# Second-layer attention with heads stacked on 32-row groups, fp32r high/low products, mask rows, and maxima in a two-bank and a one-bank region

## The reference

```python
q = (x @ wq).reshape(B, T, H, D);  lat = x @ w_down
k = (lat @ wk_up).reshape(B, T, H, D);  v = (lat @ wv_up).reshape(B, T, H, D)
q = _apply_rope(q, cos, sin);  k = _apply_rope(k, cos, sin)
scores = einsum('bqhd,bkhd->bhqk', q, k) / sqrt(D)
allowed = (arange(T) // 32)[None, :] <= (arange(T) // 32)[:, None]
attn = softmax(where(allowed, scores, finfo.min))
out = einsum('bhqk,bkhd->bqhd', attn, v).reshape(B, T, E) @ wo
```

## Time and profile before

| | us |
|---|---|
| median of the three runs shown | 2290.97 (2288.64 to 2308.19) |
| the profiled execution | 2288.33 |
| its span, first to last instruction | 2286.5 |

### The profile page before, as it was taken

How to read it: one execution, slowest core, us unless ns; L and a number is a source line. 1 busy time by engine, 2 the same in 40 slices (tenths; PEclk the granted TensorE clock), 3 DMA queues, 4 the chain that set the end, 5 groups by cost and what they waited for, 6 DMA issues and landing times. The chain is left out here.

```text
span 2286.5 us, 39722 instructions
## 1 busy us (share of the span) xinstructions
PE 1803.5 (79%) x11252; PEld 1116.8 (49%) x11300; DVE 1413.4 (62%) x2718; ACT 1200.5 (53%) x1688; POOL 496.7 (22%) x804
## 2 busy tenths in 40 slices
PE   1599999999999999742835719999899994474993
PEld 1366666666666666432832303333333333344993
DVE  4267677766676777641554448788788863522665
ACT  1478778787787777411622203556566662221441
POOL 0112211121122111105410011122122222074441
PEclk9999999999999999955966657999999997586996
DMA  4656666665566666141224541322233202511224
GB/s 168 149 143 151 157 155 156 158 146 144 143 150 157 156 156 153 40 95 49 60 63 177 176 134 32 62 52 48 54 61 61 48 15 96 72 55 49 60 61 129
DMA packets 158933, 239.46 MB, mean 105 GB/s; under 512 B 21691, under 2 KB 107932, under 8 KB 158205
## 3 DMA queue, kind: packets, MB, share of 16 engines
q1 hardware_dynamic: 148102, 222.90, 39.9%
q0 software_dynamic: 6592, 13.56, 1.8%
q10 hardware_dynamic: 4160, 2.10, 0.3%
HBM read 87.18 MB, written 50.17 MB: 60 GB/s over the span
## 5 line engine op out<-in xcount | busy, mean ns | idle before, releaser
L1012 ACT ACTIVATE a_p<-a_score 128x1024 f32<-128x1024 f32 (+3 forms) x384 | 300.7, 810 | 244.4 <-PE a_score L1029 240.4
L1118 DVE TENSOR_REDUCE a_mx<-a_misc 128x1 f32<-128x512 f32 (+3 forms) x768 | 376.3, 548 | 77.8 <-PE a_misc L1060 51.5
L438 ACT ACTIVATE a_p<-a_score 128x1024 f32<-128x1024 f32 (+3 forms) x384 | 290.4, 809 | 182.7 <-PE a_score L464 179.5
L1057 PE MATMUL a_misc<-a_k,a_q 72*128 72x512 bf16 (+3 forms) x768 | 251.7, 349 | 80.8 <-DMA a_v<-values 55.4
L464 PE MATMUL a_score<-a_q,a_kh 128*128 128x512 f32 (+3 forms) x768 | 274.9, 369 | 22.8 <-DMA a_q<-a_stage 19.4
L480 PE MATMUL a_out<-a_p,a_v 128*64 128x512 f32 (+3 forms) x1536 | 290.7, 500 | 0.0
L395 POOL TENSOR_SCALAR_AFFINE_SELECT a_p<-a_p 128x256 f32<-128x256 f32 x256 | 124.0, 514 | 719.4 <-ACT a_p L451 719.4
L451 ACT ACTIVATE a_p<-a_p 128x2560 f32<-128x2560 f32 (+1 forms) x128 | 274.6, 2145 | 1.1
L464 PE MATMUL a_score<-a_q,a_kl 128*128 128x512 f32 (+3 forms) x768 | 254.8, 348 | 0.0
L610 DVE TENSOR_TENSOR a_part<-a_part,a_p 128x1024 f32<-128x1024 f32 (+3 forms) x256 | 224.0, 875 | 8.4 <-ACT a_p L451 1.8
L1029 PE MATMUL a_score<-a_q,a_k 128*128 128x512 bf16 (+3 forms) x720 | 216.0, 327 | 1.9 <-ACT a_p L1012 1.3
(11 more groups left out here) (205 smaller groups left out, 2834.7 us busy)
## 6 DMA issues: line engine op xcount, KB each, us to landing
a_kh<-a_stage SPq DMA_DIRECT2D x128, 256.0 KB, 4.2
a_kl<-a_stage SPq DMA_DIRECT2D x128, 256.0 KB, 4.8
a_q<-a_stage SPq DMA_DIRECT2D x128, 256.0 KB, 5.5
a_xt<-xt SPq DMA_DIRECT2D x32, 512.0 KB
a_q<-qk_parts SPq DMA_DIRECT2D x144, 64.0 KB
a_k<-qk_parts SPq DMA_DIRECT2D x144, 64.0 KB
values<-p_v SPq DMA_DIRECT2D x16, 512.0 KB, 5.3
a_v<-values SPq DMA_DIRECT2D x16, 512.0 KB
```

The source lines that it names most:

```text
L438: nc.scalar.activation(chunk_of(prob[p], c), score_ps[:, c % 2, :, 0:width], ACT.Tanh, scale=scale / clamp).then_inc(tanh_done, 1)
L1012: nc.scalar.activation(prob[s % RING][:, :, 0:width], score_ps[:, s % 2, :, 0:width], ACT.Exp, scale=scale).then_inc(exp_done, 1)
L1057: mm = nc.tensor.matmul(misc[:, bank, 0:keys], q_st[bn][0:ROWS, h, t * P:(t + 1) * P], k_st[bn][0:ROWS, h, key0:key0 + keys], start=True, ...
L1118: nc.vector.tensor_reduce(m[c][:, h, t:t + 1], misc[:, bank, 0:keys], AX_X, ALU.max).then_inc(free, 1)
```

## The change

Queries and keys are split into two parts, high and low, in fp32r (fp32 storage that TensorE takes in one pass) instead of three in bf16. Three products are kept: high by high, high by low, low by high. That is 24 rows a head, then two rows for the maximum's high and low part, then three mask rows: in the keys' stack row g is one for keys of page g+1 or later of each block of 128, in the queries' stack it is a large negative number for the queries of page g. GpSimd makes these eight fixed rows once in `project1` and stores them to DRAM with eight DMAs. A head takes 32 rows, so a quad fills 128 partitions, each head on a row group of its own, and a unit's loads are two DMAs of 512 KB and one of values. Scores and maxima are matmuls on 24 + 2 or, where the mask cuts, 24 + 2 + 3 rows; a block on the diagonal is a matmul of its own of 128 columns. The GpSimd masks and the identity matmuls are gone.

Maxima use two regions instead of three banks in turn: 14 jobs of two heads in two banks, reduced by one VectorE instruction of 1024 elements, and 12 jobs of one head in one bank, which also takes the transposes. VectorE waits per region. Values are multiplied in pairs of chunks, every fourth slot, one pair behind; the exponentials have eight buffers. The output is written by one VectorE instruction per half into an array ordered by quad, and `project_out1` copies it in another order. The load of the stacks waits for the scores, that of the values for the value matmuls.

```diff
-PARTS = 3
+PARTS = 2
+PRODUCTS = ((0, 0), (0, 1), (1, 0))
+MAX_ROW = len(PRODUCTS) * DH1
+MASK_ROW, MASKS = MAX_ROW + PARTS, P // PAGE - 1
+STACK = 32
...
-                        for a in range(PARTS):
-                            dst = of(parts_dram, b)[i * PARTS + a]
-                            sp.dma_start(dst, part[i][:, a, :]).then_inc(stored, 16)
+                        for n, product in enumerate(PRODUCTS):
+                            rows = of(stack_dram, b)[i].rearrange("g (h r) t -> (g h) r t", r=STACK)
+                            sp.dma_start(rows[:, n * DH1:(n + 1) * DH1, :], part[i][:, product[i], :].bitcast(F32))\
+                                .then_inc(stored, 16)
...
+                for i in range(2):
+                    nc.gpsimd.memset(fixed[i][:], float(i)).then_inc(fixed_made, 1)
+                pool.wait_ge(fixed_made, 2)
+
+                nc.gpsimd.affine_select(out=view[0], in_=view[0], compare_op=ALU.not_equal, fill=NEGATIVE, base=PARTS,
+                                        pattern=by_page, channel_multiplier=-1).then_inc(fixed_made, 1)
+                nc.gpsimd.affine_select(out=view[1], in_=view[1], compare_op=ALU.is_ge, fill=0.0, base=PARTS - 1,
+                                        pattern=by_page, channel_multiplier=-1).then_inc(fixed_made, 1)
+                pool.wait_ge(fixed_made, 4)
+                for b in range(BATCH):
+                    for i in range(2):
...
+                        rows = stack_dram[b, i].rearrange("g (h r) t -> r (g h) t", r=STACK)
+                        pool.dma_start(rows[MAX_ROW:STACK], fixed[i][:].to_broadcast([STACK - MAX_ROW, HEADS1, SEQ]))\
+                            .then_inc(fixed_stored, 16)
...
-                        act.wait_ge(rest_done, b * 2 + i + 1)
-                        nc.scalar.copy(part[i][:, 1, :], rest[:]).then_inc(mid_done, 1)
...
-                        nc.vector.tensor_tensor(rest[:], t_cos[:], part[i][:, 0, :], ALU.subtract)\
-                            .then_inc(rest_done, 1)
-                        dve.wait_ge(mid_done, n + 1)
-                        nc.vector.tensor_tensor(part[i][:, 2, :], rest[:], part[i][:, 1, :], ALU.subtract)\
+                        nc.vector.tensor_tensor(part[i][:, 1, :], t_cos[:], part[i][:, 0, :].bitcast(F32), ALU.subtract)\
                             .then_inc(lo_done, 1)
...
+    def jobs(region, pieces):
+        step = 2 if region == WIDE else 1
+        return [(region, range(h, h + step), pieces) for h in range(0, QUAD, step)]
+
+    wide_jobs = [job for pieces in ([(0, 3, 0)], [(2, 4, 0)], [(2, 5, 0)], [(2, 6, 0)], [(2, 7, 0)], [(1, 7, 1)],
+                                    [(0, 1, 0), (1, 5, 1)]) for job in jobs(WIDE, pieces)]
+    narrow_jobs = [job for pieces in ([(0, 0, 0), (1, 4, 1)], [(0, 2, 0)], [(1, 6, 1)]) for job in jobs(NARROW, pieces)]
+    W, N = iter(wide_jobs), iter(narrow_jobs)
+    early_jobs = [next(W if k == "w" else N) for k in "wwnwwnn"]
+    rest_jobs = [next(W if k == "w" else N) for k in "wnwnwnwnwwnwnwnwnwn"]
...
+            todo = []
             if exists(u + 1):
-                left = PIECES if isinstance(u, int) and u == -1 else PIECES[EARLY:]
-                for n, piece in enumerate(left):
-                    by_slot[n * MAX_SLOTS // len(left)].append(("max", (1, *piece), n == len(left) - 1))
-                by_slot[MAX_SLOTS + 2].append(("turn_max", None, None))
-            if exists(u + 2):
-                for n, piece in enumerate(PIECES[:EARLY]):
-                    by_slot[MAX_SLOTS + n * (SLOTS - MAX_SLOTS) // EARLY].append(("max", (2, *piece), False))
+                jobs = (early_jobs if first else []) + rest_jobs
+                todo = [("max", (1, *job), n == len(jobs) - 1) for n, job in enumerate(jobs)]
             if exists(u - 1):
-                by_slot[9].append(("turn_out", 1, None))
+                todo.insert(min(9, len(todo)), ("turn_out", 1, None))
+            for n, use in enumerate(todo):
+                slot = n * MAX_SLOTS // len(todo)
+                by_slot[max(slot, 6) if use[0] == "turn_out" else slot].append(use)
+            todo = [("max", (2, *job), False) for job in early_jobs] if exists(u + 2) else []
+            if exists(u + 1):
+                todo.insert(min(1, len(todo)), ("turn_max", None, None))
             if exists(u):
-                by_slot[15].append(("turn_out", 0, None))
-            n = sum(map(len, by_slot.values()))
-            return by_slot, n
-
-        FULL = len(PIECES) + 3
-
-        def bank_of(u, at):
-
-            short = FULL - uses(u)[1] if isinstance(u, int) and u < 1 else 0
-            return (at + short) % BANKS
+                todo.insert(min(5, len(todo)), ("turn_out", 0, None))
+            for n, use in enumerate(todo):
+                by_slot[MAX_SLOTS + n * (SLOTS - MAX_SLOTS) // len(todo)].append(use)
+            return by_slot
...
+        def load_rows(sp, n, b3):
             if not exists(n):
                 return
-            kit.ge_apart(sp, pv_chunks, (n - BUFS + 1) * NCH)
-            batch, quad = (n >> 2) & (BATCH - 1), n & (QUADS - 1)
-            src = of(parts_dram, batch)
+            kit.ge_apart(sp, scored, (n - BUFS + 1) * SLOTS)
+            src = of(stack_dram, (n >> 2) & (BATCH - 1))
             for which, st in ((0, q_st), (1, k_st)):
-                for a in range(PARTS):
-                    row0 = a * (PARTS * DH1)
-                    for b in range(PARTS):
-                        part = a if which == 0 else b
-                        rows = src[which * PARTS + part].rearrange("(g h d) t -> g d h t", g=QUADS, h=QUAD)
-                        sp.dma_start(st[b3][row0 + b * DH1:row0 + (b + 1) * DH1, :, :], of(rows, quad))\
-                            .then_inc(st_loaded[b3], 16)
-            sp.dma_start(v_st[b3][:], of(of(v_dram, batch), quad)).then_inc(st_loaded[b3], 16)
+                sp.dma_start(st[b3][:].bitcast(F32), of(src[which], n & (QUADS - 1))).then_inc(st_loaded[b3], 16)
+
+        def load_values(sp, n, b3):
+            if not exists(n):
+                return
+            kit.ge_apart(sp, pv_pairs, (n - BUFS + 1) * ROUNDS)
+            sp.dma_start(v_st[b3][:], of(of(v_dram, (n >> 2) & (BATCH - 1)), n & (QUADS - 1))).then_inc(v_loaded[b3], 16)
...
-        def pool_step(pool, u, b3, d3):
-            if not exists(u):
-                return
-            for i in DIAG:
-                for hp in range(2):
-                    slot = 2 * i + hp
-                    kit.ge_apart(pool, exp_done, u * SLOTS + slot + 1)
-                    blk = prob[slot % RING][:, :, 0:P].rearrange("p h (g q) -> p h g q", q=PAGE)
-
-                    nc.gpsimd.affine_select(out=blk, in_=blk, compare_op=ALU.is_ge, fill=0.0, base=PAGE - 1,
-                                            pattern=[[0, 2], [PAGE, P // PAGE], [0, PAGE]], channel_multiplier=-1)\
-                        .then_inc(masked, 1)
...
-    RING = 6
-    PV_LAG = 2
+    RING = 8
+    ROUNDS = NCH // 2
...
+            diagonal = P if j // (TILES // 2) == half else 0
+            for a, b, last_row in ((0, diagonal, MASK_ROW + MASKS), (diagonal, width, MASK_ROW)):
+                if a == b:
+                    continue
+                for h2 in range(2):
+                    row = STACK * (2 * hp + h2)
+                    mm = nc.tensor.matmul(score_ps[:, s % 2, h2, a:b], k_st[b3][row:row + last_row, j * P:(j + 1) * P],
+                                          q_st[b3][row:row + last_row, q0 + a:q0 + b], start=True, stop=True)
+            mm.then_inc(scored, 1)
...
+        def pe_pv(pe, m, b3, pair, loads):
+            if pair == 0:
+                pe.wait_ge(v_loaded[b3], 16 * loads)
+            pe.wait_ge(exp_done, m * SLOTS + 4 * pair + 4)
+            for i in (2 * pair, 2 * pair + 1):
+                half, j, width, _ = CHUNKS[i]
+                if j == 0:
+                    ge(pe, out_evac[1 - half], m + half)
+                last_j = max(c[1] for c in CHUNKS if c[0] == half)
+                for h in range(QUAD):
+                    slot = (2 * i + h // 2) % RING
+                    mm = nc.tensor.matmul(out_ps[h * V_COLS:(h + 1) * V_COLS, HALF - width:HALF],
+                                          v_st[b3][:, j, h, :], prob[slot][:, h % 2, 0:width],
+                                          start=j == 0, stop=j == last_j)
+            mm.then_inc(pv_pairs, 1)
...
-            ge(pe, free, number if isinstance(u, int) and at < BANKS else number - (BANKS - 1))
+            back = back_to_same_region(u, at)
+            if back is not None:
+                ge(pe, free, number - (back - 1))
...
+                            bank = narrow_ps[:] if region == NARROW else wide_ps[:, h % 2, :]
+                            mm = nc.tensor.matmul(bank[:, n * keys + a:n * keys + b],
+                                                  q_st[bn][row:row + last_row, t * P:(t + 1) * P],
```

(22 more changed lines are left out.)

249 lines of the change are left out of this document (110 added, 139 removed).

## The result

The changed kernel takes 2497.3 us (median of 4, 2490.7 to 2501.5) against 2293.8 us (median of 4): ratio 1.087, interval 1.082 to 1.093. It is slower, by more than my range allowed. The profiled execution after took 2498.3 us, its span is 2496.6. These are its busy shares and granted clock, in forty slices.

A forecast was written before the change was run, and what follows sets the result against it. TensorE was taken to bound the loop, with VectorE close behind. From the profiled 2288.3 us, 16 x (34.0 - 31.4) = +42 for the loop, -17 opening and -6 projection gave 2307 us, range 2225 to 2430.

The forecast's parts named there:

- the forecast: Whole kernel: mixed clock in the second layer's attention loop, 34.0 us a unit, 2307 us in all; chance 0.45.
- Opening: Start of second-layer attention: first maxima 17 us earlier through less clearing and fewer loads; net -17 us, bounds -10 to -20.
- Projection: Stage before attention: fewer conversion steps shorten four iterations by 2.1 us each, larger stores add 2; -6 us, bounds -12 and +8.
- Loop, the pairs of values: Attention loop: 6 shape turns a unit instead of 12, 1.2 us instead of 2.4; ScalarE's wait for pairs costs nothing.
- My second price: Attention loop: ScalarE loses 0.7 us a round to a pair of chunks if its slack is gone.
- Loop, the clock: Attention loop: clock falls to 1.2 GHz in slots 0 to 14, rises in 15 to 23; 34.0 us a unit against 31.4.
- the sign that I had named: Attention loop: granted clock between 0.6 and 0.85, low where no values stand, would show the mixed-clock forecast.
- the first part: Slots 0 to 14 of a loop unit: 21.5 us at half clock, 18.7 at full, a third at full clock.
- 1 (clock holds): Attention loop: clock stays full, 29.5 us a unit; 2225 to 2235 us in all, faster; chance 0.25.
- 2 (half clock nearly throughout, 39.5 a unit): Attention loop: no block of values is long enough to raise the clock; +107 us, 2395 in all; chance 0.18.
- 3: Attention loop: pairs of heads do not run together; 2291 us at full clock, up to 2547 at half; chance 0.12.
- The risk that I named: Attention loop: VectorE's waits for the single two-bank region much longer than 0.3 to 0.7 us, making VectorE the bound.

The follow-up runs named there:

- fixed_spread: The changed kernel with the fixed rows' constant first spread over 128 partitions and stored from there, head groups outermost: 2449.5 us, ratio 1.067.
- undo_pairs: fixed_spread with the values multiplied chunk by chunk in six buffers, as before the change: 2409.5 us, ratio 1.050 against the old kernel.
- regions_only: The old kernel with only the maxima's two-bank and one-bank regions and heads written by quad; values chunk by chunk, six buffers: 2297.1 us, ratio 0.997.

## Why the prediction was wrong

The likeliest single class, slower, was right; the size was 2307 for 2497. Of the 191 us between the forecast and the profiled execution, 62 are the projection, 6 the opening, 121 the loop (163 measured, 42 booked) and 2 lie elsewhere. Step by step.

**Opening**, booked at -17 (bounds -10 to -20): -10.7. The first reduction came 5.9 us after the stage's start (forecast 6), a wide one took 1.23 us (1.2). VectorE's waits for the refill were 0.43 and 0.89 us instead of my 0.3 and 0.7, at half clock. The earlier start brought 17.8 us; 5.4 were lost again because the first unit's 26 reductions lasted 30.4 us (26.5 forecast, 25.0 before), and 1.7 with the row of maxima.

**Projection**, booked at -6 (bounds -12 and +8): +55.6, a failed step. It was "the 4.2 MB of GpSimd 13 us of transfers, in the first iteration, where the queues are slack". I priced the bytes at the stage's rate of 320 GB/s and never asked from how many partitions they are read. Read from eight partitions they moved at 45 to 51 GB/s and held SyncE's stores up with them. With the source on 128 partitions, in `fixed_spread`, the stage costs +2.5 us (attention from 1340.4 against 1337.9), inside my bounds; the other order of the destination is not ruled out as the cause. The iteration of 22.9 us (22 forecast) was right.

**Loop, the pairs of values**, booked as 1.2 us a unit saved on turns and, for ScalarE, "a pair holds TensorE 1.7 us, ScalarE has up to 2 us of work queued by then and 12 us of slack a unit: nothing, and 0.7 us a round if the slack is gone". A failed step. The pair does hold TensorE 1.71 us, and 3.2 at half clock, but 0.4 us of work was queued, and the slack of a unit is no slack in a chain in which scores and exponentials wait for each other through two buffers. Without packing the pairs cost 4.1 us a unit (35.9 against 31.9), 63 us of loop, most of it in slots 15 to 23 (13.9 against 10.5 us). My second price, 0.7 us in each of six rounds, is 4.2; I had put it behind a condition that I never tested. That the chain of scores and exponentials is what passes the stall on is argued from the rows of slots 7 and 8, not isolated.

**Loop, the clock.** The step held in kind: the four kernels with fewer rows show that rows take the clock, and 0.63 lies in the band of 0.6 to 0.85 that I gave for the forecast. So did the sign that I had named, low where no values stand. Its size did not, and that is the third failed step: I gave a third of the first part and two thirds of the second to full clock, and they had 16% and 39%. By my own prices these shares make 21.1 and 15.5 us, 36.6 a unit instead of 34.0; measured are 24.5 and 17.9. So of the 8.4 us that a unit is over the forecast, 2.6 are the clock's shares and 5.8 are prices that were too low. I had priced the unit at 40 with half clock throughout; the measured 42.4 at 0.63 is above even that. Of the 163 us the pairs are 63 and the regions -3 (499.5 against 502.9), which leaves 104 for the packing with its clock. Without pairs the same packing costs 132 (631.3 against 499.5), so the parts don't add. What of this is half clock and what is waiting on VectorE's wide region stays open: no packed kernel ran at full clock, and padding the rows to raise it brought costs of its own. One price was too low for certain: I took a pair of heads at what one costs, and it lasts 0.50 us against 0.39 in the records.

**Rivals.** 1 (clock holds) fell with the clock. 2 (half clock nearly throughout, 39.5 a unit) had the mechanism of `undo_pairs` (0.54, 40.4 us), not of the changed kernel. 3 fell with the starts 3 to 9 ns apart. The risk that I named as VectorE's waits for the two-bank region was, in `regions_only`, no cost. My range ended at 2430 because every case took the projection within +8 and the pairs as free (and the forecast's own range, 32 to 36.5 us a unit with the stage bounds added, is 2266 to 2368 and not 2268 to 2355, which would not have saved it): without the 48 us that `fixed_spread` and the 40 that `undo_pairs` gave back in turn, the kernel ran in 2409.5, inside it.

## What to carry to other kernels

Price a transfer by the partitions that it reads and the order in which it writes, not only by its bytes: the constant on eight partitions that was broadcast to memory was slow on either queue. Before merging two blocks on the engine that feeds another, look at the narrowest slot beside it and ask how much work the fed engine has in hand there; a unit's total slack doesn't answer that. Packing small matmuls onto row groups can be done and does overlap, but where the old kernel's matmuls on 72 and 128 rows ran at 2.4 GHz, the saved columns may be paid back through the clock: measure the rows alone first, in the old kernel. And look at how often neighbouring matmuls change their number of rows.

## What the runs showed of the hardware

With scores, maxima and masks on 32 rows TensorE stayed at 1.2 GHz for the loop's 859 us, though busy for 856 of them; on 64 rows it did so for all but the last 30 of 842 us. The same columns on 128 and 72 rows ran at 0.98. Scores padded with zeros from 26 to 128 rows raised the clock from 0.62 to 0.73, but TensorE's busy share rose with it, from 85 to 95%, so that zero rows count is not shown. Changing between 32 rows and more cost about 0.1 us a change at full clock (36.7 against 30.7 us a unit) and 0.29 us a slot at half. Two 26-row matmuls of 512 columns on different row groups started 3 to 9 ns apart and lasted 0.50 us together. Stores of 4 KB packets from eight partitions took 1.15 us a packet on GpSimd's queue where those from 128, written in another order, took 0.16.
